# Flamingo block in fp16 pairs: the first mixture of experts on tokens sorted by expert

## The reference

```python
x = x + tanh(g_xattn[0]) * L0_xattn(layernorm(x), ctx)     # 16 heads of 16
x = x + tanh(g_ffn[0])   * L0_ffn(layernorm(x))            # below
x = x + tanh(g_xattn[1]) * L1_xattn(layernorm(x), ctx)     # 16 heads of 64, LoRA, 4 extra keys
x = x + tanh(g_ffn[1])   * L1_ffn(x)                       # shared expert + 8 routed, top 2
# L0_ffn
xn = layernorm(x) * ln_gamma + ln_beta
abel_out = gelu(xn @ abel_w + abel_b)
topw, topi = top_k(xn @ moe_gate_w + moe_gate_b, 2)        # softmax over the two
h = gelu(einsum('bsd,edh->ebsh', xn, ew1) + eb1)           # 8 experts, 256 -> 512
eo = einsum('ebsh,ehd->ebsd', h, ew2) + eb2                # 512 -> 256
moe_out = einsum('ebsd,bse->bsd', eo, w_dense)             # w_dense: 0 but for the top 2
for i in range(3):
    moe_out = moe_out @ expm(gens[i])                      # 256 x 256
gate = sigmoid(concat([abel_out, moe_out]) @ gc_w + gc_b)
return x + abel_out * (1 - gate) + moe_out * gate
```

## Time and profile before

| | us |
|---|---|
| median of 3 runs | 1166.42 |
| fastest and slowest of them | 1162.39, 1167.53 |
| the profiled execution, its time | 1168.22 |
| its span in the profile | 1166.5 |
| TensorE busy (7407 matmuls) | 961.9 (82%) |
| VectorE busy | 736.9 (63%) |
| ScalarE busy | 514.4 (44%) |
| GpSimd busy | 405.5 (35%) |
| chain that ended last: TensorE, VectorE, ScalarE, issue | 55%, 23%, 9%, 9% |

### The profile page before, as it was taken

How to read it: one execution, slowest core, us unless ns; L and a number is a source line. 1 busy time by engine, 2 the same in 40 slices (tenths; PEclk the granted TensorE clock), 3 DMA queues, 4 the chain that set the end, 5 groups by cost and what they waited for, 6 DMA issues and landing times.

```text
span 1166.5 us, 20990 instructions
## 1 busy us (share of the span) xinstructions
PE 961.9 (82%) x7407; PEld 698.7 (60%) x7407; DVE 736.9 (63%) x1496; ACT 514.4 (44%) x1004; POOL 405.5 (35%) x408
## 2 busy tenths in 40 slices
PE   0699999998298999978528899999999966899990
PEld 0488888887264455566424567666776655566660
DVE  5465666664739888887784676777777754343332
ACT  3254555554132343354324565565566542124330
POOL 1598778770314566500020233322332210500005
PEclk9899999998569899998769999999999995889995
DMA  6433323220121131142200011111110137411213
GB/s 194 155 101 108 90 72 90 72 72 2 72 69 52 53 102 67 55 136 77 72 0 25 20 38 37 38 37 37 36 36 26 47 110 250 156 32 51 63 38 104
DMA packets 53601, 84.42 MB, mean 72 GB/s; under 512 B 5121, under 2 KB 41097, under 8 KB 51618
## 3 DMA queue, kind: packets, MB, share of 16 engines
q1 hardware_dynamic: 48978, 77.16, 20.7%
q0 software_dynamic: 1536, 3.67, 1.1%
q10 hardware_dynamic: 3024, 2.75, 0.7%
HBM read 60.99 MB, written 22.57 MB: 72 GB/s over the span
## 4 chain that ended last, share of the span: by engine, by line
PE 55%; DVE 23%; ACT 9%; issue 9%; DMA 2%; POOL 1%; DVEq 0%; ACTq 0%; POOLq 0%
PE tp L709 6%; PE sp L695 6%; PE pb L651 5%; PE pb L1301 5%; PE pb L726 4%; PE sp L1612 3%; PE tp L1612 3%; PE pb L1642 3%; PE pb L672 2%; DVE ST L952 2%; PE sp L1286 2%; PE tp L1286 2%; DVE ST L955 2%; PE pb L645 2%; ACT ST L831 2%
## 5 line engine op out<-in xcount | busy, mean ns | idle before, releaser
L838 ACT ACTIVATE ST<-tp 125x672 f32<-125x672 f32 (+1 forms) x128 | 93.5, 730 | 152.5 <-PE tp L709 152.4
L695 PE MATMUL sp<-KT,qz 128*112 128x375 f16 (+1 forms) x768 | 119.4, 335 | 16.1 <-ACT ST L831 13.6
L709 PE MATMUL tp<-identf,ST 112*125 112x112 f32 x768 | 114.4, 286 | 9.8 <-ACT ST L828 7.8
L709 PEld LDWEIGHTS tp<-identf,ST 112*125 112x125 f32 x768 | 97.3, 191 | 38.3 <-ACT ST L828 17.5
L1394 POOL TENSOR_TENSOR qz<-qz,Z 128x448 f32<-128x448 f32 x64 | 86.0, 1364 | 92.3 <-ACT qz L1329 92.2
L1091 POOL TENSOR_TENSOR ST<-pn,sums 112x8 f32<-112x8 f32 x64 | 13.0, 204 | 256.5 <-ACT ST L831 256.5
L695 PEld LDWEIGHTS sp<-KT,qz 128*112 128x112 f16 (+1 forms) x768 | 68.3, 130 | 45.4 <-ACT ST L831 16.7
L952 DVE TENSOR_SCALAR_CACHE_REDUCE ST<-sp 112x375 f32<-112x375 f32 x128 | 65.0, 545 | 37.0 <-PE sp L695 34.8
L828 ACT ACTIVATE ST<-ST,nm 112x375 f32<-112x375 f32 x128 | 70.7, 600 | 38.1 <-DVE ST L955 37.7
L1028 POOL TENSOR_SCALAR Z<-Z 128x512 f32<-128x512 f32 x54 | 83.5, 1547 | 3.8 <-DMA Z<-in_moe 3.6
L1301 PE MATMUL pb<-V,KT 128*128 128x448 f16 x384 | 77.6, 360 | 6.5 <-DVE V L1373 6.5
(11 more groups left out here) (272 smaller groups left out, 2038.3 us busy)
## 6 DMA issues: line engine op xcount, KB each, us to landing
Z<-in_moe SPq DMA_DIRECT2D x54, 256.0 KB, 3.1
cut_scratch<-Z SPq DMA_DIRECT2D x54, 256.0 KB, 2.4
ST<-in_moe SPq DMA_DIRECT2D x8, 1024.0 KB, 6.7
W<-cut_scratch SPq DMA_DIRECT2D x32, 128.0 KB, 4.1
Z<-wd_scratch SPq DMA_DIRECT2D x8, 448.0 KB, 4.6
KT<-cut_scratch SPq DMA_DIRECT2D x8, 384.0 KB, 6.4
V<-cut_scratch SPq DMA_DIRECT2D x8, 384.0 KB, 7.0
ST<-in_ctxT SPq DMA_DIRECT2D x4, 750.0 KB, 5.7
```

The costliest lines, as they stand in the source:

```text
L695: mm = pe.matmul(SB_[j][0:S, 0:L.keys], q, kT[bs % 2][qb][r, t, 0:L.keys], start=(n == 0), stop=(n == 2))
L709: mm = pe.transpose(TB_[j][0:CHUNK, c * S:(c + 1) * S], P_[:, st % 2, j, c * CHUNK:(c + 1) * CHUNK], identf[0:S, 0:S])
L838: act.activation(PT[:, st % 2, :, 0, :] if l else PT0[:, st % 2, :, :], TP2[0:CHUNK, :, 0:NCH * S], ACT.Copy)\
```

## The change

The first mixture is computed on sorted tokens with the same machinery as the second.

- **Routing of the first layer** (`route_vector(dve, 0)`): two best experts, ranks, slots. The softmax weights are kept for each of the two places.
- **Weights** of the first mixture become 32 more pieces (`PIECES0` = 4 for each of 8 experts; three steps each on GpSimd), stored cut in DRAM, and loaded whole (8 MB) into W1, KT and V once they are. In all there are 86 pieces: 44 in the first attention (`FIRST_LAYER`, the 32 among them), 12 beside the tiles (`ROUTED`), 30 in the second attention, whose 90 steps are spread over its 64 patches (26 patches have two).
- **The row traffic** (`rows0_gpsimd`, `tiles0_sync`, `combine0_vector`): 16 indirect scatters, a load for each tile, a store for each tile, 16 indirect gathers, 16 combining passes of VectorE.
- **Tiles** (`tiles0_tensor`, `tiles0_scalar`, `tiles0_vector`): 21 tiles of 128 slots. The tile's rows are turned and cut, `up(i)` has 24 matmuls of 128 columns, four Gelus add the owner's bias from `tile_bias` (which `bias_tensor` picks with a product by a one-hot matrix), VectorE cuts, `down(i)` has 14 matmuls of 256 columns, and the product is copied out and stored.
- **The exponentials' units**: 12 Horner units (`HEAD`) run between the router and the tiles, 9 in the tiles, one for two tiles, and the remaining 16 after them. All thirty VectorE items stand there now, two for a unit from place 22. The first steps (`expm_first_*`) run before the routing instead of beside the dense experts.
- `gate_abel_vector` and `residual_abel_vector` stand behind tiles 3 and 5 on VectorE.
- Behind the exponentials the combined rows, which lie token by token, are turned (`turn_tensor(pe, 2, Y, ...)`) for the product with them; `moved_scalar` and `moved_vector` go.
- Removed: `expert_order`, `experts` and its five functions, `weights_tensor`, `weights_scalar`, `biases_*`.
- BT, R16, RT, RF and LD change their place in SBUF.

The diff, cut to its core (a line "..." marks what is left out):

```diff
-FIRST_BETWEEN = 6
+FIRST_BETWEEN = 22
...
-CUTS = (E + 1) * PIECES
-CUTS0 = 36
+PIECES0 = 4
+CUTS0 = E * PIECES0
+CUTS = CUTS0 + (E + 1) * PIECES
+FIRST_LAYER, ROUTED = 44, 12
+HEAD = 12
...
+        HOMES0 = [(W1F, 0, 0, 4), (KT, 1, 0, 3), (VF, 1, 3, 1)]
...
+                    for n in range(STEPS1 * i // (B * NP), STEPS1 * (i + 1) // (B * NP)):
+                        piece_gpsimd(pool, FIRST_LAYER + ROUTED + n // 3, n % 3)
...
+        def bias_tensor(pe):
+            pe.transpose(pb[0][0:E * NM, 0:128], b1[:, :, :].rearrange("p e m -> p (e m)"), identf[:, :])\
+              .then_inc(s["bias_mm"], 1)
+            pe.wait_ge(s["bias_set"], 1)
+            pe.wait_ge(s["sel_set"], 4)
+            pe.matmul(pb[1][:, 0:NM * NT], b1T[:, :], sel[:, :, :].rearrange("p m i -> p (m i)"), start=True, stop=True)\
+              .then_inc(s["bias_mm"], 1)
+        def bias_vector(dve):
+            dve.wait_ge(s["bias_mm"], 1)
+            dve.tensor_copy(b1T[:, :], pb[0][0:E * NM, 0:128]).then_inc(s["bias_set"], 1)
+            dve.wait_ge(s["bias_mm"], 2)
+            dve.tensor_copy(tile_bias, pb[1][:, 0:NM * NT]).then_inc(s["bias_set"], 1)
...
+            def up(i):
+                if i == 0:
+                    pe.wait_ge(s["owner_set"], 1)
+                    pe.wait_ge(s["routed_in"][0], 16 * len(HOMES0) * E)
+                    pe.wait_ge(s["bias_set"], 2)
+                owner_of[i] = pe.value_load(owner_i[0:1, i:i + 1], min_val=0, max_val=E - 1)
+                pe.wait_ge(s["x_lo"], i + 1)
+                if i >= 2:
+                    pe.wait_ge(s["h_act0"], i - 1)
+                for m in range(NM):
+                    n = 0
+                    for k in range(2):
+                        for qa, qb in PARTS:
+                            w = block0_of[qa, k][:, bass.ds(owner_of[i] * PIECE + m * 128, 128)]
+                            mm = pe.matmul(pb[i % 2][:, m * SLOTS:(m + 1) * SLOTS], w, xsT0[:, i % 2, qb, k, :],
+                                           start=(n == 0), stop=(n == 5))
+                            n += 1
+                mm.then_inc(s["up_mm0"], 1)
...
+            def down(i):
+                pe.wait_ge(s["h_lo"], i + 1)
+                if i >= 2:
+                    pe.wait_ge(s["y_rd"], i - 1)
+                dst = YB[i % 2][:, 0:C]
+                for q in range(2):
+                    if i == 0 and q == 0:
+                        pe.wait_ge(s["sel_set"], 4)
+                    pe.matmul(dst, bc(sel16[:, i:i + 1], [E, SLOTS]), eb2[:, q, :], start=(q == 0), stop=False)
+                n = 0
+                for k in range(NM):
+                    for qa, qb in PARTS:
+                        w = block0_of[qb, 2 + k // 2][:, bass.ds(owner_of[i] * PIECE + k % 2 * C, C)]
+                        mm = pe.matmul(dst, hTs0[:, i % 2, qa, k, :], w, start=False, stop=(n == 3 * NM - 1))
+                        n += 1
+                mm.then_inc(s["y_mm"], 1)
+            for i in range(2):
+                turn_x(i)
+            for i in range(NT + 2):
+                if i < NT:
+                    up(i)
+                if i + 2 < NT:
+                    turn_x(i + 2)
+                if i >= 2:
+                    down(i - 2)
+                expm_tensor(pe, units_beside(i))
+        def units_beside(i):
+            return range(min(HEAD + i // 2, HORNER), min(HEAD + (i + 1) // 2, HORNER))
...
+            for i in range(NT + 3):
+                if i < NT:
+                    act.wait_ge(s["up_mm0"], i + 1)
+                    if i >= 2:
+                        act.wait_ge(s["h_lo"], i - 1)
+                    for m in range(NM):
+                        x = act.activation(hf0[:, i % 2, m * SLOTS:(m + 1) * SLOTS],
+                                           pb[i % 2][:, m * SLOTS:(m + 1) * SLOTS], ACT.Gelu,
+                                           bias=tile_bias[:, m * NT + i:m * NT + i + 1], scale=1.0 / WS)
+                    x.then_inc(s["h_act0"], 1)
+                if i + 2 < NT:
+                    cut_x0_scalar(act, i + 2)
+                if 2 <= i < NT + 2:
+                    give(i - 2)
+                if i >= 3:
+                    store(i - 3)
+                if i < NT + 2:
+                    expm_scalar(act, units_beside(i))
...
+        def tiles0_vector(dve):
+            for i in range(2):
+                cut_x0_vector(dve, i)
+            for i in range(NT + 2):
+                if i < NT:
+                    dve.wait_ge(s["h_act0"], i + 1)
+                    if i >= 2:
+                        dve.wait_ge(s["y_mm"], i - 1)
+                    hi = hTs0[:, i % 2, 0, :, :].rearrange("p k n -> p (k n)")
+                    dve.tensor_scalar(hi, hf0[:, i % 2, :], HS, None, ALU.mult).then_inc(s["h_hi"], 1)
+                    dve.wait_ge(s["h_hi"], i + 1)
+                    dve.scalar_tensor_tensor(hTs0[:, i % 2, 1, :, :].rearrange("p k n -> p (k n)"), hf0[:, i % 2, :],
+                                             HS, hi, ALU.mult, ALU.subtract).then_inc(s["h_lo"], 1)
+                if i + 2 < NT:
+                    cut_x0_vector(dve, i + 2)
+                expm_vector(dve, units_beside(i))
+                if i == 3:
+                    gate_abel_vector(dve)
+                if i == 5:
+                    residual_abel_vector(dve)
...
+        def rows0_gpsimd(pool):
+            pool.wait_ge(s["zero_out"], 16)
+            pool.wait_ge(s["slot_set"], 1)
+            for b in range(B):
+                for n, _ in places0(b):
+                    pool.indirect_dma_start(xs_dram[:, :], bass.IndirectOffsetOnAxis(ap=slot_u[:, n:n + 1], axis=0),
+                                            Z[:, b, :], None).then_inc(s["scattered"], 16)
+            pool.wait_ge(s["scattered"], 16 * 2 * B)
+            for n in range(FIRST_LAYER, FIRST_LAYER + ROUTED):
+                for part in range(3):
+                    piece_gpsimd(pool, n, part)
+            for parity in range(2):
+                pool.wait_ge(s["ys_out"][parity], 16 * ((NT + 1 - parity) // 2))
+            pool.wait_ge(s["mix"], B + 3)
+            for b in range(B):
+                for n, dst in places0(b):
+                    pool.indirect_dma_start(dst, None, ys_dram[:, :],
+                                            bass.IndirectOffsetOnAxis(ap=slot_u[:, n:n + 1], axis=0))\
+                        .then_inc(s["back_in"][b], 16)
+        def combine0_vector(dve, b):
+            if b == 0:
+                dve.wait_ge(s["rt_sm_0"], 3)
+            dve.wait_ge(s["back_in"][b], 32)
+            (_, first), (_, second) = places0(b)
+            dve.tensor_scalar(first, first, w12[:, 0, b:b + 1], None, ALU.mult).then_inc(s["moe_row"], 1)
+            dve.wait_ge(s["moe_row"], 2 * b + 1)
+            dve.scalar_tensor_tensor(first, second, w12[:, 1, b:b + 1], first, ALU.mult, ALU.add)\
+               .then_inc(s["moe_row"], 1)
+        def tiles0_sync(sp):
+            def rows_in(i):
+                if i >= 3:
+                    sp.wait_ge(s["x_mm"], i - 2)
+                sp.dma_start(xs0[:, i % 3, :], xs_dram[i * SLOTS:(i + 1) * SLOTS, :]).then_inc(s["xs_in"][i % 3], 16)
+            sp.wait_ge(s["scattered"], 16 * 2 * B)
+            for i in range(3):
+                rows_in(i)
+            n, last = FIRST_LAYER, FIRST_LAYER + ROUTED
+            piece_fetch(sp, n)
+            piece_fetch(sp, n + 1)
+            for i in range(3, NT):
+                rows_in(i)
+                if i % 3 and n < last:
+                    piece_store(sp, n)
+                    if n + 2 < last:
+                        piece_fetch(sp, n + 2)
+                    n += 1
+            while n < last:
+                piece_store(sp, n)
+                n += 1
...
-        for place, (what, n, j) in enumerate(order, FIRST_BETWEEN):
+        for item, (what, n, j) in enumerate(order):
+            place = FIRST_BETWEEN + item // 2
             BETWEEN["vector"].setdefault(place, []).append((what, n, j))
             if what == "add":
...
+                for b in range(B):
+                    if n == len(EU) - 11 + b + b // 2:
+                        combine0_vector(dve, b)
...
-            experts_sync(sp, 0, E)
-            sp.wait_ge(s["m_lo_0"], 2 * E)
             for j in range(2):
                 sp.dma_start(ST[:, j, 0:3 * 512], a["gens"][j, :, :]).then_inc(s["e_in"], 16)
+            pieces_stored(sp, CUTS0)
+            for e in range(E):
+                for home, q, c, n in HOMES0:
+                    dst = home[:, 0:n * BLK].rearrange("p (c m) -> p c m", c=n)[:, :, e * PIECE:(e + 1) * PIECE]
+                    sp.dma_start(dst, cut0_dram[e, :, q, c:c + n, :]).then_inc(s["routed_in"][0], 16)
+            tiles0_sync(sp)
+            for parity in range(2):
+                sp.wait_ge(s["ys_out"][parity], 16 * ((NT + 1 - parity) // 2))
...
-            experts_scalar(act, 0, E, "first")
             turn_scalar(act, 1)
+            expm_first_scalar(act)
```

(30 more changed lines are left out.)

570 lines of the change are left out of this document (203 added, 367 removed).

## The result

Over 20 runs each, the changed kernel took 1161.78 us in the median (1149.45 to 1177.87) and the one before 1167.70 us: ratio 0.9921, 95% interval 0.9896 to 0.9946. It is 0.8% faster, where 3.8% had been forecast; 1161.8 lies just above the stated range of 1093 to 1158. Ratios and their intervals leave out executions that took over 1.5% more than the fastest of their kernel; medians are over all.

What follows compares the result with a forecast made beforehand. TensorE bounds both attentions; the prizes were TensorE work in the first mixture's experts and engines idle beside the exponentials. 1168.2 - 47.5 gained there + 3 in the attentions = 1123.7, or 1122 us for the median; range 1093 to 1158.

Steps and rivals of the forecast that it cites:

- The rest of the exponentials: Last down-product to the product with the exponentials: late start, VectorE's work and idle time 67.6 us, transposing 2.9; 70.5 forecast.
- The late start: After the tiles: store landing 3 us, first weights about 4, ScalarE's cut 1.7, so VectorE's items start at +9.
- The start of the tiles: End of the first attention to the first up-product: 72.9 us forecast, with the first up-product at 364 us.
- rival (c): TensorE starves of instructions in the new tiles, about 9 us a stretch; seven stretches give 1185 us; chance 0.05.
- high end: Top of the range, 1158 us: rival (b)'s 20, one starved stretch of 9 and 7 of the attentions' bounds.
- Contention in the tiles: In the first mixture's tiles, GpSimd's pieces slow VectorE's passes: 6 us within the forecast 98 us of tiles.
- Rival (b): VectorE and GpSimd exclude each other all through the tiles, 26 us in place of 6: 1142 us; chance 0.15.
- VectorE's gate and residual at tiles 3 to 5: Some 13 us of VectorE in the tiles, about 5 hidden by two buffers; 8 us taken as stalling the tiles.
- First attention: Eight more pieces on GpSimd still fit; dearer clips beside them cost at most 3 us, 1 taken.
- Second attention: 90 cut steps instead of 54 over 64 patches cost 0 to 8 us, 2 taken.
- the four terms of the loop: VectorE's high, low and cut, then transposes and down in a tile: 1.1 + 0.4 + 0.2 + 1.5, given as 3.3 us.
- 0.92: Chance that the whole kernel gets faster by over 0.5%: the forecast and rivals (a), 1093 us, and (b) together.

Runs made afterwards that it cites:

- e6: Changed kernel with four PSUM banks instead of two for the LoRA products: median 1146.52 us against 1155.19 on the same chip, ratio 0.9745 to the kernel before.
- e3: Changed kernel with filler matmuls into an unused bank behind the last sixteen units and each LoRA product: ratio 0.9823 to the kernel before.

## Why the prediction was wrong, step by step

- **The rest of the exponentials** is the step that failed: "Before, VectorE idled 14 us of 56 here, about 0.6 a unit; I keep that, 9 us, though every item's product now waits for an add of the same unit." That clause was the mechanism and got no price. The program of TensorE has, in order, a unit, its two LoRA products and the next unit. With two banks a product waits for the add two before, which stands behind ScalarE's and VectorE's steps of the unit just issued. So the steps of a unit lie end to end, and two banks in place of four cost 7.5 to 8.2 us (e6). The late start was "+9"; VectorE's first item came at 497.5, +12.6, and the products waited until 506.4 because the factors pass three cuts first; loading two chunks earlier gave 4 us. 81.1 in place of 70.5; with both mended, 67.0 to 68.5. In this chain a unit of twelve matmuls takes 2.77 us at 1.2 GHz and 1.47 at full clock, which the prediction did not price either; no run shows what that costs.
- **The start of the tiles** was right within 2.6 us where no stretch came (74.6 to 75.5 for 72.9). Where it came, 7 to 11 us more: rival (c)'s own mechanism, once instead of five times. The prediction held it for a rare accident of an unrolled step ("once in 29") and put one stretch only into its high end; it comes with sixteen scatters on some chips, and the change has a second set of them. The kernel before had been profiled on such a chip, and "with scatters running" stood beside the row, so one more stretch belonged in the sum.
- **Contention in the tiles** was taken at 6 us and measured 6 to 8 (95.1 to 96.6 without pieces); with it the tiles were 102.8 for 98, and the other 3 to 5 us are not accounted for. Rival (b), whole-instruction exclusion at 26 us, did not come in that size. Of the rule in the Trainium skill, SBUF — State Buffer, § Who interferes with whom, the trace shows the sign: 692 to 925 ns in the low pass, 427 to 534 in the high one, on average a third and a quarter longer. It agrees with the page in the four low passes of 1.52 or 1.53 us that waited for GpSimd's step; what (b) had wrong is how often that comes, four passes of eighteen. VectorE's gate and residual at tiles 3 to 5 did stall TensorE, as said (6.5 us of waits from 400 to 423 us, the longest 4.0).
- **First attention**: "I take 1", at most 3; 5.2 in the profile and 7.1 in the mean of eleven, but 1 to 2 at a like granted clock. The prediction left out that this stage's length moves with the clock by more than its bound.
- **Second attention**: "I take 2"; nothing (348.6 to 358.3 us, before 351.3 and 351.4). The 2.6 over the forecast in the profile goes with its clock, 0.96 against 0.98 before; the 1.7 ahead of it and the 1.2 behind are not accounted for.
- Small slips of its sums are under 1 us each and decide nothing: 9 + 49.4 + 9 is 67.4, not 67.6; the 16 units have 16 low passes, not 15; the four terms of the loop add to 3.2, not 3.3; 18 tiles at 1.4 us are 25, not 26.
- The sign was right, as 0.92 had it; the size was not, since the three largest misses (the start of the tiles, the tiles, the end part) lie on one path and add.

## What to carry to other kernels

When two items are put where one was, follow the in-order engine that feeds both: if its buffers are as many as the items, the item's consumer ends each unit, and twice the buffers cost little where banks are free (here two banks and one wait). Put background work beside a stage that has room for it, here the second attention (162 steps free) and not the tiles (6 to 8 us for 12 pieces). And before trusting a stage's length from one profile, see it on a second chip, and compare it at a like granted clock.

## What the runs showed of the hardware

- Sixteen indirect scatters in a row held up TensorE's and ScalarE's next instructions for about 10 us in all nine profiles of some chips (the first ones of before and after among them), and not at all in the eight profiles of two others with the same scatters; where they were put off on a chip of the first kind (one profile), the units beside which they had stood ran without a gap. How the scatters do it is not shown: the profile calls the idle time "issue" or "remote".
- The granted clock can stay at 1.2 GHz although TensorE is busy by the rows: 0.50 from 325 to 345 us with 18.95 of 20 us busy, behind 3.4 us of idle time, transposes with gaps of 0.7 and 1.3 us, and products of 8 columns. Fillers that raised the clock of the end part from 0.62 to 0.95 left its length as it was (e3: 81.1 and 82.1 us), but they took time of their own there.
- The two attentions' lengths go with the granted clock more than with the steps beside them: the first ended at 301.4 to 306.1 us at 0.92 to 0.93 and at 288.3 to 296.3 at 0.95 to 0.98; the second took 348.6 to 348.9 us at 0.99 and 351.3 to 358.3 at 0.96 to 0.98.
- A two-operand pass of VectorE over 512 columns took 0.69 us, and 1.52 or 1.53 where it began within 0.4 us behind the start of GpSimd's two-operand step of 1.2 to 1.4 us, ending 0.54 or 0.55 us behind that step.
